# Down's ten tile pairs in seven products for eight, with the activation sums made by VectorE

## The reference

```python
gate = lora_add(einsum('bnh,fh->bnf', x, W_gate), x, A_gate, B_gate)   # F = 2752 = 21.5 x 128
up   = lora_add(einsum('bnh,fh->bnf', x, W_up), x, A_up, B_up)
act  = silu(gate) * up
x = x + lora_add(einsum('bnf,hf->bnh', act, W_down), act, A_down, B_down)   # "Down"
x = x + einsum('bsi,oi->bso', x, weight) + bias + scale * (x @ a_sel.T) @ b_sel.T
```

## Time and profile before

| | us |
|---|---|
| median of the runs | 1643.05 |
| profiled execution | 1642.49 |
| its span, first to last instruction | 1640.8 |
| TensorE busy | 1609.4 (98%) |
| VectorE, GpSimd, ScalarE busy | 1069.9, 727.0, 554.2 |

### The profile page before, as it was taken

How to read it: one execution, slowest core, us unless ns; L and a number is a source line. 1 busy time by engine, 2 the same in 40 slices (tenths; PEclk the granted TensorE clock), 3 DMA queues, 4 the chain that set the end, 5 groups by cost and what they waited for, 6 DMA issues and landing times.

```text
span 1640.8 us, 21154 instructions
## 1 busy us (share of the span) xinstructions
PE 1609.4 (98%) x7060; PEld 1313.4 (80%) x7060; DVE 1069.9 (65%) x1198; ACT 554.2 (34%) x969; POOL 727.0 (44%) x529
## 2 busy tenths in 40 slices
PE   6999999999999999999999999999999999999998
PEld 4778888888888788888888788888888887778886
DVE  5777777766668777776665655566655577855433
ACT  3744444444447444444444211111111121431110
POOL 5565555555555555555555453323332321641110
PEclk9999999999999999999999999999999999999999
DMA  8434534533443334334224932112222221113322
GB/s 157 106 94 106 147 101 107 148 81 92 118 109 85 110 106 144 104 106 135 81 80 129 303 98 81 59 51 81 80 67 66 68 66 27 24 23 81 79 53 52
DMA packets 218127, 156.13 MB, mean 95 GB/s; under 512 B 110692, under 2 KB 200164, under 8 KB 215268
## 3 DMA queue, kind: packets, MB, share of 16 engines
q1 hardware_dynamic: 169536, 114.92, 27.5%
q10 hardware_dynamic: 48356, 39.86, 7.7%
q0 software_dynamic: 128, 0.00, 0.0%
HBM read 115.38 MB, written 39.32 MB: 94 GB/s over the span
## 4 chain that ended last, share of the span: by engine, by line
PE 91%; SPq 3%; issue 2%; DVE 2%; ACT 1%; DMA 1%; POOL 1%; DVEq 0%; ACTq 0%
PE ps L1971 91%; SPq L1199 1%; DMA Ad_raw<-in_L_cond_A_down_dram 1%; ACT Bf L1466 1%; SPq L1285 1%; POOL Bf L1886 0%; SPq L470 0%; DVE acc L932 0%; DVE tw_down L940 0%; SPq L1216 0%; SPq L1191 0%; POOL W L1834 0%; SPq L1267 0%; DVE Ad_turned L899 0%; SPq L1163 0%
## 5 line engine op out<-in xcount | busy, mean ns | idle before, releaser
L1971 PE MATMUL ps<-act,Wd 128*128 128x512 f32 x2016 | 462.5, 389 | 1.6 <-POOL Wd L1901 1.5
L1971 PE MATMUL ps<-X_T,W 128*128 128x512 f32 x1944 | 455.9, 389 | 5.0 <-POOL W L1834 3.8
L1971 PEld LDWEIGHTS ps<-act,Wd 128*128 128x128 f32 x2016 | 378.3, 188 | 82.0 <-POOL Wd L1901 1.8
L1971 PE MATMUL ps<-X_B,W 128*128 128x512 f32 x1728 | 417.4, 391 | 14.3 <-ACT X_B L1408 13.5
L1971 PEld LDWEIGHTS ps<-X_T,W 128*128 128x128 f32 x1944 | 364.7, 188 | 81.8 <-issue 6.2
L1971 PEld LDWEIGHTS ps<-X_B,W 128*128 128x128 f32 x1728 | 325.8, 189 | 83.4 <-issue 14.9
L932 DVE TENSOR_TENSOR acc<-acc,ps 128x1024 f32<-128x1024 f32 x176 | 214.2, 1220 | 177.1 <-PE ps L1971 176.6
L1834 POOL TENSOR_TENSOR W<-s,W 128x512 fp32r<-128x512 f32 x156 | 211.6, 1358 | 133.0 <-ACT W L1379 130.1
L1834 POOL TENSOR_TENSOR W<-TG,W 128x512 fp32r<-128x512 f32 x88 | 128.9, 1466 | 150.4 <-ACT W L1379 150.1
L1893 POOL TENSOR_TENSOR act<-stage,act 128x1024 fp32r<-128x1024 f32 x42 | 100.6, 2413 | 175.0 <-ACT act L1618 175.0
L1379 ACT ACTIVATE W<-s 128x512 fp32r<-128x512 f32 x156 | 98.2, 632 | 217.8 <-PE ps L1971 212.1
(11 more groups left out here) (135 smaller groups left out, 1537.8 us busy)
## 6 DMA issues: line engine op xcount, KB each, us to landing
stage<-act_scratch SPq DMA_DIRECT2D x21, 1024.0 KB, 5.0
raw<-in_L_cond_W_gate_dram SPq DMA_DIRECT2D x164, 128.0 KB, 2.9
raw<-in_L_cond_W_up_dram SPq DMA_DIRECT2D x164, 128.0 KB, 3.2
raw<-in_x_dram SPq DMA_DIRECT2D x104, 128.0 KB, 2.8
raw<-in_L_cond_W_down_dram SPq DMA_DIRECT2D x88, 128.0 KB, 3.2
act_scratch<-c21buf ACTq DMA_DIRECT2D x42, 256.0 KB, 2.4
act_scratch<-vbuf ACTq DMA_DIRECT2D x42, 256.0 KB, 2.9
xt_scratch<-xt ACTq DMA_DIRECT2D x4, 2048.0 KB, 6.6
```

Source lines behind the costliest of these rows:

```text
L1971: return nc.tensor.matmul(dst, stationary, moving, start=start, stop=stop, skip_group_check=True)
```

## The change

Tiles 1 to 20 of `act` are taken as ten pairs (1,3), (2,4), (5,7), ...: for two features sets each, Down's weights are seen as two-by-two blocks, and seven products are made for eight, over all output tiles at once. Five blocks `b` of two pairs (`SEVENS`) replace blocks 0 to 9; in each, for both token halves `tp`, seven steps P1, P5, P6, P3, P7, P2, P4 of 24 matmuls, and t after P2. Both pairs of a block accumulate in PSUM. Block 10 now holds tile 0 and the half tile.

The weights' sums are made in Down by VectorE (`sum_weights`). The sums of activations, T1 to T4, are made by VectorE in the units (`make_moves`) and stored to a new scratch (`store_moves`). In Down each step loads its own moving operand into one of eight slots (`load_moving`), two steps ahead.

```diff
+            def make_moves(U):
+                if not paired(U):
+                    return
+                n = pair_number(U)
...
+                if leads(U):
...
+                    V.tensor_tensor(t_move[:, :], keep[:, :], c21buf[:, :], ALU.subtract
+                                    ).then_inc(moves.up((n, "T1")), 1)
+                    return
+                eng.wait_ge(moves.sem, moves.after((n, "T1")))
+                V.tensor_tensor(keep[:, :], vbuf[:, :], keep[:, :], ALU.subtract).then_inc(moves.up((n, "T3")), 1)
+                eng.wait_ge(t_stored, 32 * n + 16)
+                V.tensor_tensor(t_move[:, :], vbuf[:, :], t_move[:, :], ALU.subtract
+                                ).then_inc(moves.up((n, "T2")), 1)
+                eng.wait_ge(moves.sem, moves.after((n, "T2")))
+                eng.wait_ge(t4_stored, 16 * n)
+                V.tensor_tensor(t4_move[:, :], c21buf[:, :], t_move[:, :], ALU.subtract
+                                ).then_inc(moves.up((n, "T4")), 1)
...
                     second_act(U - 1)
                 add_q(U)
+                make_moves(U - 1)
                 turn_tile(("G", U + 1))
...
+                    for c in range(2 if bb < LAST else 1):
+                        if bb < LAST:
+                            groups = slice(16 * e, 16 * e + 16)
+                            first = first_group(2 * bb + 1 + c, q) * Q
+                            dst = home.rearrange("i (g c f) -> i c g f", c=2, f=Q)[:, c]
...
+                        sp.dma_start(dst, rows[:, groups, first:first + Q]).then_inc(filled, 16)
...
+            def load_ad(p):
+                if p == 0:
+                    wait_turned(sp, ("D", 1, 1))
+                else:
+                    sp.wait_ge(ad_turned, p)
                 for b in range(NB):
...
+                    for q in range(NQ):
+                        first, second = (first_group(2 * p + 1 + c, q) for c in range(2))
+                        sp.dma_start(Ad_raw[q * Q + e * R:q * Q + (e + 1) * R, place:place + 2 * Q].rearrange(
+                            "r (c i) -> r c i", c=2), groups[:, first:second + 1:second - first, :]
+                            ).then_inc(ad_loaded, 16)
...
+            def load_sevens():
+                for g, (b, tp, name) in enumerate(ALL_STEPS):
+                    n = g % len(STEPS)
+                    if 3 <= g + 2 < len(ALL_STEPS):
+                        load_moving(g + 2)
+                    if b == 0 and tp == 0 and n < 2:
+                        load_ad(n)
+                    if b < SEVENS - 1:
+                        when = (1, 5, 6, 7) if b == 0 else (1, 2, 3, 4)
+                        if 7 * tp + n in when:
+                            i = when.index(7 * tp + n)
+                            load_down(("D", 2 * b + 2 + i // 2, i % 2))
+                        if (tp, n) == (0, 6):
+                            load_ad(2 * b + 2)
+                        elif (tp, n) == (1, 2):
+                            load_ad(2 * b + 3)
...
+            def seven_step(b, tp, name):
+                item, s = USES[name][0], (b, tp, name)
+                eng.wait_ge(ws_lo.sem, ws_lo.after((b, item, 1)))
+                eng.wait_ge(moving_lo.sem, moving_lo.after(s))
+                for hh in range(2):
+                    event = (b, tp, name, hh)
+                    tile_free(event)
+                    for e in range(2):
+                        dst = ps[tile_of(event)][:, e * TT:(e + 1) * TT]
+                        for j in range(2):
+                            for wl, xl in THREE:
+                                last = matmul(dst, Ws[item][:, j, wl, 2 * hh + e, :], moving[slot_of[s]][:, xl, j, :],
+                                              start=name in FRESH and (j, wl, xl) == (0, 0, 0),
+                                              stop=(j, wl, xl) == (1, 1, 0))
+                    last.then_inc(pe_s.up(event), 1)
...
+                        elif (tp, n) == (1, 6):
+                            last_low(0)
+                            td_first(0)
+                            td_first(1)
+                            turn_item(("Bd", 1))
+                            bd_low(0)
+                            bd_low(1)
```

More of the change, by code:

```diff
@@ L102, in build @@
[L102 to L107, removed]
+        Ws = {i: at(f"Ws_{i}", o, [P, 2, 2, 4, P], F32R) for i, o in (
+            ("A11", 65536), ("S1", 73728), ("S2", 106496), ("S4", 172032), ("S3", 180224), ("A12", 188416),
+            ("A22", 196608))}
@@ new lines, in build, with released @@
+        LAST_STEP = (SEVENS - 1, 1, "P4", 1)
+        LAST_T = (SEVENS - 1, 1, "t", 0)
+        def released(s):
+            b, tp, name = s
+            return (b, tp, "t", 0) if name in T_STEPS else (b, tp, name, 1)
+        slot_of, slot_before, slot_level, holder = {}, {}, {}, [None] * len(SLOTS)
+        landings = [0] * len(SLOTS)
+        for g, s in enumerate(ALL_STEPS):
+            homes = range(6)
+            if s[:2] == (SEVENS - 1, 1):
+                homes = {"P1": (6,), "P5": (7,)}.get(s[2], (0, 1, 2, 5))
+            j = min(homes, key=lambda i: (EVENTS.index(released(holder[i])) if holder[i] else -1, i))
+            slot_of[s], slot_before[s] = j, holder[j]
+            landings[j] += 1
+            slot_level[s] = 16 * landings[j]
+            holder[j] = s
@@ L1271, in load_act @@
-            def load_act(t):
-                if t == 0:
-                    sp.wait_ge(spilled, 4 * 16)
-                elif t >= 2:
-                    for pr in range(2):
-                        sp.wait_ge(act_lo.sem, act_lo.after((t - 2, pr)))
-                for c in range(2):
-                    sp.wait_ge(act_stored[c], 16 * (UNITS + t + 1))
-                rows = P if t < FULL else HC
-                sp.dma_start(stage[t % 2][0:rows, :], act_d[t, 0:rows, :]).then_inc(stage_loaded[t % 2], 16)
@@ new lines, in seven_t @@
+            def seven_t(b, tp):
+                event = (b, tp, "t", 0)
+                tile_free(event)
+                eng.wait_ge(ad_lo, 2 * b + 2)
+                dst = ps[tile_of(event)][:, 0:TT]
+                for name, rows in (("P1", 4 * Q), ("P2", 4 * Q), ("P5", 2 * Q), ("P3", 2 * Q)):
+                    for j in range(2):
+                        if name in ("P1", "P5"):
+                            part = AE[:, tp, j, :, :, :] if name == "P1" else AE[:, tp, j, 0:1, :, :]
+                        else:
+                            part = AO[:, tp, j, 1:3, :, :] if name == "P2" else AO[:, tp, j, 0:1, :, :]
+                        for l in range(2):
+                            last = matmul(dst[0:rows, :], part.rearrange("p x l r -> p (x l r)"),
+                                          moving[slot_of[b, tp, name]][:, l, j, :],
+                                          start=(name, j, l) == ("P1", 0, 0), stop=(name, j, l) == ("P3", 1, 1))
+                last.then_inc(pe_s.up(event), 1)
```

940 lines of the change are left out of this document (624 added, 316 removed).

## The result

The changed kernel takes 1769.8 us (median of four runs, 1768.7 to 1773.8) against 1642.4 for the kernel before: ratio 1.0778, 95% interval 1.0756 to 1.0800. The forecast was 1738, its range 1670 to 1790. Direction and places came out as forecast; the term furthest off is TensorE's slow start after a wait.

A forecast was written before the change was run, and what follows sets the result against it. TensorE, busy 98% of the span, was taken as the bound. 1642.5 - 54.4 (fewer matmuls) + 31.5 (activation sums) + 102 (waits in Down) + 7 (cold TensorE) + 9.5 (last block's entry) = 1738 us; range 1670 to 1790.

The forecast's parts named there:

- 240 matmuls less: In Down, 1680 matmuls replace 1920, at 0.2267 us each: -54.4 us.
- activation sums in the units: In 18 odd units VectorE's sums behind add_q make P4 start 1.75 us late: +31.5 us; even units 0.
- waits in Down: Moving operands queue on SP behind adapter and weight loads, so TensorE waits in blocks 0 to 3: +102 us (75 to 119).
- slow matmuls after waits in Down: After waits of 8 us or more TensorE starts at its lower clock, up to 3.4 us each: +7 us (0 to 14).
- way into the last block: Entering the last block, t waits 2.7 us for last_low(0) and 7 more for VectorE's queued work: +9.5 us (2 to 16).
- The rival that they are free: In the units, VectorE makes the activation sums in its idle time and P4 isn't late: 1707 us; chance 0.22.
- Rival (3), short pieces: In Down, weight tiles in 128-byte pieces land in 6.4 us instead of 3.2, twelve waits grow: 1776 us; chance 0.12.
- two of block 0's four long waits ... 2 x 3.4 = +7 (0 to 14): In Down's block 0, two long waits cost 3.4 us of slow matmuls each; SP's next wait hides the other two.

The follow-up runs named there:

- The run with pauses: The kernel before, with TensorE stopped once in each of Down's blocks 1 to 8 by a chain of small SP DMAs: 1706.7 us, ratio 1.0390.
- the run with 8 DMAs a pair: The changed kernel with Down's adapter rows loaded by 8 DMAs a pair instead of 32, in 1792-byte pieces: 1716.3 us, ratio 1.0448.

## Why the prediction was right, and the term that was not

| term | forecast, us | measured, us |
|---|---|---|
| 240 matmuls less | -54.4 | -54.4 |
| activation sums in the units | +31.5 | +34.8 |
| waits in Down | +102 | +99.2 |
| slow matmuls after waits in Down | +7 | +31.1 |
| way into the last block | +9.5 | +17.8 |

With the 1.6 us that Down waited before the change and no longer does, these give 126.9; the spans differ by 127.0.

- **Sums in the units: right in mechanism, place and size.** 1.75 forecast, 1.80 measured, in the 18 units named; none in even ones. The run with the sums ahead of add_q shows that the order was the cause, and that the idle time was usable after all, on its other side. The rival that they are free falls.
- **Waits in Down: right in cause and nearly wait by wait; the sum is partly luck.** Block 0: 8.5 for 8.0, 13.7 for 16.8, 2.7 for 3.1, 16.7 for 18.6, 8.9 for 11.3. Blocks 1 to 3: 3.4 to 3.8 for 3.4, 7.3 to 8.0 for 6.6, 0.4 to 1.0 for 3.2, nothing for 1.5. Block 4: none. TensorE's share of the five blocks is 448.2 of 547.5 us, 82%. Missed was the first, 10.9 us: I let block 0 start as it did before and didn't ask what the accumulators, now loaded from ScalarE's queue, do to the weight tile that lands beside them; another 1.8, for VectorE ahead of an adapter sum, was not forecast either. Without these two the waits come to 86.5 against 102, so that the sum came out within 3 us is luck. Operands landed in 4.2 to 4.7 us (forecast 4.0), SP's pitch was 0.50.
- **Rival (3), short pieces, came nearest in time (1776) and is wrong.** With pieces and bytes unchanged and half the issues the batches took half the time and 23 us went. The Trainium skill ("DMA: Bandwidth & Descriptors", Specifications) asks for 512 bytes a piece for the full rate; by that the 128-byte weight tiles would be late, but their median landing was 2.5 us for 64 KB, against 3.2 for 128 KB in 256-byte pieces before.
- **The step that failed: "two of block 0's four long waits ... 2 x 3.4 = +7 (0 to 14)".** I counted only waits of 8 us and more, and let SP's next wait hide half. TensorE's busy time in Down came out 31.1 us above the full pace. The rows behind thirteen waits, from 1.9 us up, show 27.7 of it, 2.1 each; most of the rest is the 0.16 us of a row's end, once for each of seventeen waits. The run with pauses measures 2.4 by itself (16.5 over seven) and shows that it goes by the number of waits and not by their length. The granted clock right after a wait, in the middle of an undisturbed stretch, and after a 1.50 us wait in the units (columns as in the windows above):

```profile
959.72:965.20 5.48, 5.48 (x13) 4.37 (x14) 5.31 (x6) 2.21 (x3) 5.48 (x3) 0.50 0.46 153
1117.20:1139.00 21.80, 21.80 (x97) 17.83 (x95) 11.84 (x10) 1.46 (x3) 11.52 (x8) 1.00 0.27 61
910.91:913.80 2.89, 2.89 (x13) 2.37 (x14) 1.87 (x3) 0.97 (x2) 2.75 (x3) 1.00 1.01 243
```

0.50 is the lower of the two levels, 1.2 GHz; after the wait of 1.50 in the units the clock stayed at 1.00. Eleven of the thirteen were waits that the forecast had; 11 x 2.1 would have been +23 instead of +7. The Trainium skill ("TensorE: Matmul & The Clock Gate", Part 1) has the low level as the state that idleness brings back; seven of the eight pauses agree.
- **The way into the last block: right kind, half the size.** last_low(0) cost 2.87 for 2.7. The wait for Td in the first token half was 2.9 instead of 7, but the second half, which I had left out, waited 6.8 on VectorE (sums 3.2, Td 3.6; 1.1 before the change), and some 6 us are slow matmuls again.

## What to carry to other kernels

Count the waits as well as their length: a stop of TensorE of more than 3 us cost 1.4 to 3.0 us beyond itself here, whatever its length. When a layout change splits a load, price the issues on the queue (0.5 us each here, for loads of 4 KB and of 64 KB alike) and ask what stands behind them, and which landing place must be free before the next may go. Before new work on a busy engine, look on which side of its idle time it is put: the same sums cost 32.5 us behind add_q; ahead of it 26.5 us of the run's time came back.

## What the runs showed that was not expected

A weight tile of eight 64 KB loads was turned 13 us after its last load was issued, against a median landing of 2.5 us, while four loads of 1 MB from another engine's queue were in flight; issuing those later gave 9.1 us back. Loads moved to another engine's queue cost 19.8 us when they were issued four steps ahead and saved 48.4 when they were issued as their places came free (three more of the first six were left to SP, too): a wait for a landing place stopped ScalarE's casts as well. And after a wait of about 2 us TensorE was once slow and once not (1.94 and 2.04 us); the wait of 1.88 in the units was followed by a granted clock of 1.00 in the kernel before and of 0.57 in the changed one (545.67 and 562.67, first 3 us), and one of 2.83 in the run with 8 DMAs a pair by the full pace.
